# Turning the quantised weight tiles ahead of the down products in the even units of the experts' loop

## What is computed

```python
x = x + _L0_xattn_ref(_layernorm(x, axis=-1), ctx_512, ctx_512)
x = x + _L0_ffn_ref(_layernorm(x, axis=-1), classifier_w, e_score_correction_bias, gate_w, up_w, down_w)
x = x + _L1_xattn_ref(_layernorm(x, axis=-1), ctx_512, Wq, w_kc_q, w_kc_kv, W_qr, W_kr, Wo)
x = x + _L1_ffn_ref(_layernorm(x, axis=-1), w_gate, w_up, w_down)

def _L0_ffn_ref(x, ...):              # 8 experts of 128 inner units, 2 of 12 routes chosen
    g = jnp.einsum('bsh,eih->bsei', x, gate_w)
    u = jnp.einsum('bsh,eih->bsei', x, up_w)
    act = jax.nn.silu(g) * u
    expert_out = jnp.einsum('bsei,ehi->bseh', act, down_w)
    out = jnp.einsum('bse,bseh->bsh', w_full[..., :n_routed], expert_out)
    return out + x * jnp.sum(w_full[..., n_routed:], axis=-1, keepdims=True)
```

## Time and profile before

| | us |
|---|---|
| median of 3 runs | 793.93 |
| lowest and highest of them | 793.36, 794.29 |
| the profiled execution, its own time | 798.54 |
| its span in the profile | 796.8 |
| granted TensorE clock over the span | 0.983 of full speed |

### The profile page before, as it was taken

How to read it: one execution, slowest core, us unless ns; L and a number is a source line. 1 busy time by engine, 2 the same in 40 slices (tenths; PEclk the granted TensorE clock), 3 DMA queues, 4 the chain that set the end, 5 groups by cost and what they waited for, 6 DMA issues and landing times. The chain is left out here.

```text
span 796.8 us, 14991 instructions
## 1 busy us (share of the span) xinstructions
PE 737.3 (93%) x4872; PEld 537.3 (67%) x4872; DVE 594.1 (75%) x1089; ACT 403.7 (51%) x1068; POOL 563.9 (71%) x588
## 2 busy tenths in 40 slices
PE   3999999988999999789999999999999999876786
PEld 2655555447888888666877777777777777552454
DVE  5889888958787879776657676776677667449996
ACT  1678888723333233245545555455555545354464
POOL 5667777426777768377576888887888888717995
PEclk9999999979999999999999999999999999898999
DMA  9300000021001010321200000000000000000001
GB/s 246 135 2 0 0 0 1 2 98 77 21 21 39 20 59 1 110 99 51 100 1 1 2 1 1 2 2 1 1 2 1 2 2 1 1 1 7 28 30 44
DMA packets 8764, 24.14 MB, mean 30 GB/s; under 512 B 1711, under 2 KB 5167, under 8 KB 8087
## 3 DMA queue, kind: packets, MB, share of 16 engines
q1 hardware_dynamic: 8154, 23.28, 8.9%
q10 hardware_dynamic: 549, 0.08, 0.1%
HBM read 21.26 MB, written 2.10 MB: 29 GB/s over the span
## 5 line engine op out<-in xcount | busy, mean ns | idle before, releaser
L1744 POOL TENSOR_TENSOR q<-turned 64x512 f32<-64x512 f32 x128 | 167.9, 1311 | 24.2 <-DVE turned L1670 11.3
L1413 PE MATMUL ps<-l_yt,a 128*128 128x512 f32 x576 | 142.6, 398 | 4.0 <-DVE a L1624 2.3
L1413 PEld LDWEIGHTS ps<-l_yt,a 128*128 128x128 f32 x576 | 104.8, 188 | 27.9 <-DVE a L1624 2.9
L1731 POOL TENSOR_TENSOR p<-p,l_inverse 128x512 f32<-128x512 f32 x64 | 66.4, 1040 | 65.2 <-DVE l_inverse L1692 64.4
L1670 DVE TENSOR_TENSOR turned<-ps,rope 128x1024 f32<-128x1024 f32 x64 | 78.0, 1219 | 39.8 <-PE ps L1413 30.0
L880 PE MATMUL ps<-yt_experts,wsplit 128*128 (+1 forms) x384 | 97.3, 403 | 0.1
L467 DVE TENSOR_REDUCE negmax<-ps 128x4 f32<-128x512 f32 x128 | 85.1, 686 | 14.8 <-PE ps L290 13.6
L1566 ACT ACTIVATE p<-ps,l_negmax 128x128 f32<-128x128 f32 x256 | 89.9, 389 | 4.9 <-DVE l_negmax L1661 4.9
L880 PEld LDWEIGHTS ps<-yt_experts,wsplit 128*128 128x128 f32 x384 | 71.6, 193 | 14.5 <-DVE inner L1035 0.3
L383 ACT ACTIVATE pt<-ps 128x512 f32<-128x512 f32 x128 | 69.8, 599 | 5.5 <-PE ps L312 3.7
L1583 ACT ACTIVATE qs<-ps 128x512 f32<-128x512 f32 x32 | 19.1, 597 | 104.6 <-PE ps L1430 104.6
(11 more groups left out here) (225 smaller groups left out, 1592.4 us busy)
## 6 DMA issues: line engine op xcount, KB each, us to landing
wide<-in_wide SPq DMA_DIRECT2D x8, 768.0 KB, 4.4
mx_raw<-in_mx SPq DMA_DIRECT2D x8, 384.0 KB, 3.1
x<-in_x SPq DMA_DIRECT2D x4, 512.0 KB, 9.3
ctx_t<-in_ctx_t SPq DMA_DIRECT2D x1, 2048.0 KB, 7.9
out<-x SPq DMA_DIRECT2D x16, 128.0 KB, 1.7
narrow<-in_narrow SPq DMA_DIRECT2D x8, 192.0 KB, 4.2
ktraw<-in_ctx_rows SPq DMA_DIRECT2D x1, 1248.0 KB
wraw<-in_gate SPq DMA_DIRECT2D x1, 1024.0 KB, 18.9
```

Of the source, the lines that this page charges most:

```text
L1413: out = pe.matmul(tile_bank(n, k), a[i][:, pa, kin, k * 128:(k + 1) * 128], yt[j % 2][:, py, kin, :, :].rearrange("p b s -> p (b s)"), sta ...
L1731: pool.tensor_tensor(p[:, head, :, :], p[:, head, :, :], spread(inverse[:, head, :], 2, S), ALU.mult).then_inc(normed[head], 1)
L1744: t = pool.tensor_tensor(out[rows[(head + half) % 2], head, :], turned[rows[head], half, :], turned[rows[head], 2 + half, :], ALU.add)
```

## The change

The block with the three transposes, its two waits and its semaphore stands ahead of the down products instead of behind them. No instruction, wait, buffer or count is added or removed.

```diff
@@ -896,6 +896,14 @@
                 if first and u == 2:
                     routes(1)
                     routes(2)
+                if x % 2 == 0 and inside(u - 2 - LEAD, UNITS):
+                    c = 4 * j + x // 2 - 1
+                    pe.wait_ge(mx_made, c)
+                    pe.wait_ge(h_made, u - 1)
+                    for i in range(3):
+                        t = pe.transpose(mx_ps[:, i * 128:(i + 1) * 128],
+                                         quantised[(x // 2) % 2][:, i * 128:(i + 1) * 128], m.ident16[:, :])
+                    t.then_inc(mx_turned, 1)
                 if inside(u - 3, UNITS):
                     expert = (x - 3) % EXPERTS
                     pe.wait_ge(h_lo, u - 2)
@@ -908,14 +916,6 @@
                                           start=(expert == 0 and q == 0 and s % 2 == 0),
                                           stop=(expert == EXPERTS - 1 and q == 2 and s % 2 == 1))
                     t.then_inc(down_made, 1)
-                if x % 2 == 0 and inside(u - 2 - LEAD, UNITS):
-                    c = 4 * j + x // 2 - 1
-                    pe.wait_ge(mx_made, c)
-                    pe.wait_ge(h_made, u - 1)
-                    for i in range(3):
-                        t = pe.transpose(mx_ps[:, i * 128:(i + 1) * 128],
-                                         quantised[(x // 2) % 2][:, i * 128:(i + 1) * 128], m.ident16[:, :])
-                    t.then_inc(mx_turned, 1)
```

## The result

The changed kernel takes 810.01 us (median of 4 runs, 809.4 to 811.87) against 794.11 us before (median of 4, 793.36 to 799.58), 15.9 us more; the ratio is 1.0185, 95% interval 1.0153 to 1.0218. It was timed again beside the experiments: 810.5 us (6 runs) against 793.97 (17 runs), ratio 1.0207, interval 1.0174 to 1.0241. The forecast was 810.1. How far runs of one kernel lie apart goes with the clock that they were granted: among these 17 runs the kernel before took 792.4 us at a mean clock of 0.994 (6 runs) and 795.1 at 0.987 (4 runs).

The account below looks back on a forecast made before the run. TensorE's queue was taken to pace the experts' units, so the newly exposed wait for h costs in full: 10.6 + 5.0 + 0.6 = 16.2 us on 793.93 gives 810.1 us, range 806.8 to 813.7.

Parts of the forecast that it names:

- The bound: Experts' units: TensorE's own queue paces them, so a microsecond it stands still there is a microsecond of the kernel.
- The plain unit: Ten even units such as unit 18: 5.72 us from one L894 to the next against 4.66, +1.06 each, +10.6 together.
- The small terms: TensorE's restart after h: wake-up 0.06, exposed first transpose load 0.05, slower start of the products behind 0.10 us.
- Rival 1: Loads of transposes and down products run ahead during the wait, so 0.05 and 0.10 vanish: 808.0 us; chance 0.09.
- rival 2: TensorE restarts dearer after each wait, from 0.25 us more per unit: 813.6 and up, 815.0 at 0.35; chance 0.07.
- Units x = 4: Units 12, 20 and 28, where VectorE's h is late: 6.59 us against 4.93, +1.66 each, +5.0 together.
- unit 4: First unit with x = 4, where down products waited 0.87 us for GpSimd: 6.37 against 5.79 us, +0.6.
- The 0.24: Units 12, 20, 28: h ends 0.24 us later against TensorE, which reaches the next L894 sooner without transposes between.
- Not slower: Rival: the transposes' wait is already met by the product of the step before; 793.3 us, chance 0.03.
- That chain: Last stretch, 318.4 to 331.0 us: TensorE's 4.0 us idle follows L894 of unit 31, so nothing is given back.
- rival 3: Experts' stage: idle pieces make the granted clock fall to 0.83, 30 us more, 840 us; chance 0.04.
- the sign: What would show the forecast in the changed kernel's profile: among others, the clock stays at 1.00.

Follow-up runs that it names:

- the wait alone: Kernel before with one wait added: in even units the down products wait for h, transposes stay behind them; 809.51 us, ratio 1.0192.
- the two runs with part of the cover: Changed kernel with the transposes behind the first 8, or the first 4, of the 12 down products: 797.33 us and 803.13 us.
- the third trace: The changed kernel traced again without an edit: 812.48 us for this single execution, its stage 140.25 us.
- the last experiment: Kernel before with GpSimd's reciprocal deviation moved from unit 31 to the end of the last stretch: 797.37 us, ratio 1.0034.

## Why the prediction was right, point by point

**The bound.** TensorE's queue paced the stage, and its idle time went to the stage in full: 15.9 us more without a fall of the clock. That the wait does it is shown by the wait alone, by the two runs with part of the cover and by the run with the transposes ahead and no wait.

**The plain unit.** Forecast 5.72 us, measured 5.65 to 5.74. The small terms (0.06 wake-up, 0.05 load, 0.10 slow start) add up rightly: from the end of h to the next L894 unit 18 takes 273.92 - 269.37 = 4.55 (h ran from 268.68 for 0.69 us). One by one they are off by a few hundredths that cancel: 0.15 us to the first transpose instead of 0.11, 0.13 for the transposes instead of 0.15, 1.52 to the gates instead of 1.54. Rival 1 (loads run ahead of the wait, 5.57) and rival 2 (a dear restart, 6.0) both fall by the unit's time, and rival 1 by the load as well: it starts at 269.49, 0.12 us after h has ended, and not during the wait.

**Units x = 4.** Forecast 6.59, measured 6.60 to 6.62 where no fall of the clock lies in it; unit 28 had 6.31 to 6.33, where I had let it stand as 6.59. That makes 4.8 to 4.9 for the three instead of 5.0. The ten plain units make 10.4 instead of 10.6, unit 4 0.6 as forecast. The 0.24 is shown by the pair of runs with and without these units.

**Unit 4.** Forecast 6.37, measured 6.34 to 6.36.

**Not slower.** The wait was not met, in any of the 14 places.

**Two steps that failed, of opposite sign.** "That chain starts from L894 of unit 31, so it moves along and absorbs nothing" was wrong. The chain of the last stretch started from GpSimd's deviation and tile, and VectorE waited 0.88 us for it; TensorE's delay in unit 30 gives GpSimd that time. It gave back 0.97 us, shown by the last experiment. And rival 3, with 4 chances in 100, came about on a small scale: not the stage at 0.83, but one fall of 1.6 us in two of three executions, where the sign was to be a clock of 1.00.

**Luck in the number.** The stage of the third trace is 15.9 us longer, against my 16.2; less what the last stretch gave back it is 14.9. At equal clock the timed runs say the same: of the runs timed side by side, those at a mean clock of 0.987 took 809.9 us (2 runs) against 795.1 (4 runs), 14.8 more. The medians differ by 15.9 and 16.5, since the median clock of the changed kernel was 0.987 and that of the kernel before 0.991; the falls behind unit 12, in two traces of three, are part of that. So 810.1 and 810.0 agree to 0.1 us because the forecast was 1.3 us too high for the idle time and had nothing for the clock, and because of where few runs happened to fall: the interval of the ratio reaches from 13.8 to 19.1 us.

## What to carry to other kernels

When an instruction is moved ahead, look at what its waits count, and whether the event is made by the instruction that now stands just before it: then every engine's round trip between the two is exposed, and everything behind it in that queue pays. The price can be read from the trace of before, as the end of the awaited work less the start of the instruction that triggers it, plus the restart. Where two tiles share a bank, the shared bank is the dependence: with another bank the order was free.

## What the runs showed of the hardware

- Behind a wait for VectorE TensorE's first load started 0.12 us after the end of h and the first transpose 0.15 us after it (unit 18). The down products behind took 1.52 us to the gates instead of 1.44. Together that is 0.2 us beyond the work itself, and the ten plain units lie within 0.07 us of the 5.72 that it makes.
- A wait of 1.8 us in the middle of dense work had a fall of the clock to 1.2 GHz behind it in two of three executions, which cost 1.6 us each time, and behind waits of the same length at unit 20 (1.81 to 1.82 us) it had none. What decides it is open.
- VectorE's quantising steps with their scratch values on SBUF instead of PSUM took longer beside GpSimd: 0.18 us on PSUM and up to 0.90 on SBUF for the step on 12 elements, 0.57 and up to 1.33 for one on 384. The kernel with that move took 16.4 us more, as much as the change itself. That I had not expected.
